# Mixture-of-experts slots behind cross-attention: two slots between stages, twelve row buffers, plans moved or split, and sends ahead of scatters on POOL

## The reference

```python
def _L0_xattn_ref(src, tgt, src_mask, tgt_mask, W_src, b_src, W_tgt, b_tgt, W_out, b_out):
    ...
    scores = jnp.einsum('bthd,bshd->bhts', q, k) / np.sqrt(HEAD_DIM)
    scores = jnp.where(src_mask[:, None, None, :] == 0, -jnp.inf, scores)
    attn = jax.nn.softmax(scores, axis=-1)
    tgt_update = jnp.einsum('bhts,bshd->bthd', attn, v).reshape(b, t, OUT_SIZE)
    cat_tgt = jnp.concatenate([tgt, tgt_update], axis=2)
    return jnp.einsum('btf,of->bto', cat_tgt, W_out) + b_out
def _L0_ffn_ref(x, router_w, w1, w2):
    ...
    probs = jax.nn.softmax(xf @ router_w.T, axis=-1)
    topv, topi = jax.lax.top_k(probs, 2)
    topv = topv / (topv.sum(axis=-1, keepdims=True) + 1e-09)
    cw = (jax.nn.one_hot(topi, e, dtype=xf.dtype) * topv[..., None]).sum(axis=1)
    h = jax.nn.gelu(jnp.einsum('td,edh->teh', xf, w1), approximate=False)
    y = jnp.einsum('teh,ehd->ted', h, w2)
    out = jnp.einsum('te,ted->td', cw, y)
...
x = x + jnp.tanh(g_xattn[0]) * _L0_xattn_ref(ctx_2048, _layernorm(x, axis=-1), mask_BxS2_fk1, ...)
x = x + jnp.tanh(g_ffn[0]) * _L0_ffn_ref(_layernorm(x, axis=-1), ...)
```

## Time and profile before

| | us |
|---|---|
| median of 3 executions | 447.37 (446.19 to 448.81) |
| the profiled execution, whole | 448.54 |
| its span, first to last instruction | 446.7 |
| PE busy | 369.7 (83%) |
| DVE busy | 227.2 (51%) |
| ACT busy | 183.3 (41%) |
| POOL busy | 268.4 (60%) |
| mean granted clock of PE | 0.938 |

### The profile page before, as it was taken

One profiled execution on the slowest core, in us unless ns is written; L12 is line 12 of the kernel. 1 busy time (PEld: TensorE's weight loads), 2 busy tenths in 40 slices (PEclk: granted clock), 3 DMA queues, 4 the chain that ended last, 5 costly groups with the idle time before them and its releaser, 6 DMA issues.

```text
span 446.7 us, 9992 instructions
## 1 busy us (share of the span) xinstructions
PE 369.7 (83%) x3067; PEld 304.4 (68%) x3067; DVE 227.2 (51%) x884; ACT 183.3 (41%) x428; POOL 268.4 (60%) x355
## 2 busy tenths in 40 slices
PE   0699999998999999999547878769766999999960
PEld 0566666676666667676336768769766999999960
DVE  1435345667778687777571534324225333365323
ACT  2164544554554555544323524423222444444420
POOL 2446354642787878868350785775855665677560
PEclk9899999998999999999855999989968999999995
DMA  7213330202122111760112121221212223743306
GB/s 212 64 38 116 117 112 26 71 25 61 32 71 63 44 47 44 194 133 25 51 54 54 56 61 55 72 61 52 75 51 81 66 69 105 238 116 111 82 13 212
DMA packets 44323, 36.04 MB, mean 81 GB/s; under 512 B 5426, under 2 KB 40151, under 8 KB 44272
## 3 DMA queue, kind: packets, MB, share of 16 engines
q1 hardware_dynamic: 35504, 24.83, 20.2%
q0 software_dynamic: 4544, 8.47, 5.7%
q10 hardware_dynamic: 4224, 2.10, 1.7%
HBM read 22.82 MB, written 13.47 MB: 81 GB/s over the span
## 4 chain that ended last, share of the span: by engine, by line
PE 67%; issue 14%; DVE 6%; POOL 4%; DMA 4%; SPq 1%; another core or an unknown queue 1%; ACT 1%; DVEq 0%; POOLq 0%
PE ps_ts L1245 17%; PE ps_proj L1256 8%; PE ps_o L1256 8%; PE ps_st L1085 5%; PE ps_st L1088 5%; PE ps_o L1176 3%; PE ps_proj L1132 3%; PE ps_proj L1136 2%; PE ps_ts L1102 2%; DVE x2n L998 2%; PE ps_tail L1163 2%; PE ps_ts L1106 2%; PE ps_tail L1154 2%; DMA maskn<-mask 2%; DVE tw L848 1%
## 5 line engine op out<-in xcount | busy, mean ns | idle before, releaser
L1245 PE MATMUL ps_ts<-xt,w1c 128*128 128x128 f32 x624 | 87.7, 286 | 10.4 <-issue 8.2
L1245 PEld LDWEIGHTS ps_ts<-xt,w1c 128*128 128x128 f32 x624 | 79.8, 200 | 12.1 <-issue 9.2
L598 POOL DMA_INDIRECT picked<-yo,xg x78 | 79.0, 1013 | 13.1 <-POOL pscratch L588 8.5
L710 ACT ACTIVATE probT<-ps_ts 128x512 f32<-128x512 f32 x78 | 46.5, 597 | 66.2 <-PE ps_ts L1245 43.4
L565 POOL DMA_INDIRECT rows<-xr,posi x64 | 63.3, 989 | 16.1 <-issue 15.8
L539 POOL TENSOR_TENSOR kblk<-kT,headcol 128x512 fp32r<-128x512 f32 x32 | 33.3, 1040 | 52.5 <-ACT kT L645 52.3
L588 POOL TENSOR_TENSOR pscratch<-minus_half 1x1 f32<-1x1 f32 x102 | 26.9, 264 | 54.1 <-DVE yo L1041 49.9
L946 DVE TENSOR_REDUCE rowmax<-ps_ts 128x8 fp32r<-128x1024 f32 x32 | 39.1, 1221 | 36.5 <-PE ps_ts L1106 36.5
L1088 PEld LDWEIGHTS ps_st<-negident,rowmax 128*128 128x128 f32 x256 | 30.9, 189 | 24.3 <-issue 24.3
L632 ACT ACTIVATE probT<-ps_st,pencol 128x1024 f32<-128x1024 f32 x32 | 35.6, 1113 | 27.7 <-PE ps_st L1088 27.0
L1256 PE MATMUL ps_o<-w2s,probT 128*128 x312 | 43.2, 283 | 4.3 <-issue 4.3
(11 more groups left out here) (141 smaller groups left out, 626.1 us busy)
## 6 DMA issues: line engine op xcount, KB each, us to landing
xg<-rows SPq DMA_DIRECT2D x78, 65.0 KB
ctxs<-ctxT SPq DMA_DIRECT2D x32, 128.0 KB, 2.1
xs<-x SPq DMA_DIRECT2D x8, 256.0 KB
w1s<-w SPq DMA_DIRECT2D x4, 512.0 KB, 3.6
w2s<-w SPq DMA_DIRECT2D x8, 256.0 KB
maskbc<-picked SPq DMA_DIRECT2D x4, 512.0 KB
out<-xs ACTq DMA_DIRECT2D x8, 256.0 KB
maskbc<-mask SPq DMA_DIRECT2D x6, 256.0 KB
```

The costliest lines, as they stand in the source:

```text
L598: nc.gpsimd.indirect_dma_start(out=picked, out_offset=bass.IndirectOffsetOnAxis(ap=xg[:, r, D + 1:D + 2].bitcast(I32), axis=0), in_=yo[:, ...
L710: nc.scalar.activation(hid[:, j % 2, :, :], heads(ps_score[j % 2][:, :]), ACT.Gelu).then_inc(f_gelu, 1)
L1245: last = nc.tensor.matmul(ps_score[j % 2][:, c * 128:(c + 1) * 128], w1c[:, j % 2, c * 128:(c + 1) * 128], xt[:, j % XRING, :], start=True ...
```

## The change

- `RING` goes from 8 to 12; the register batches stay at eight (`REGS`).
- `LAG_UP` goes from 1 to 2 and `LAG_DOWN` from 2 to 4. `w1c`, `ps_score` and `hid` have three buffers (`DEEP`); the third `ps_score` is a half of `ps_st`, the others of `hid` come from the second half of `probT`'s heads. `ps_y` and the banks of T stay at two. `each_slot` runs two slots more to drain.
- plan(0) stands at the end of DVE's step (9, 1), plan(1) is cut in four pieces that run before slots 33, 34, 35 and 36.
- SP's second pads are issued one by one, each behind a load of slots 39 to 46.
- In the mixed steps POOL runs the three slots' sends first and the step's own work, the scatters, second.

```diff
-RING = 8
+RING = 12
+REGS = 8
 XRING = 4
-LAG_UP = 1
-LAG_DOWN = 2
+LAG_UP = 2
+LAG_DOWN = 4
+DEEP = 3
...
+PLAN_AT = PER * (GROUP * (DRAINED - TAIL) - 1)
...
-def each_slot(step, slot):
+def each_slot(step, slot, slots_first=False):
...
-            step(g, k)
+            if not slots_first:
+                step(g, k)
             for j in range(j, j + PER):
                 slot(j)
             j += 1
+            if slots_first:
+                step(g, k)
...
-        w1c = sb("w1c", [128, 2, HID])
+        w1c = sb("w1c", [128, DEEP, HID])
...
-        hid = probT[:, :, 0:HCH, :]
+        hid = probT[:, :, :, :].rearrange("p r (a c) t -> p (r a) c t", c=HCH)
...
-        ps_score = [ps_ts[:, 0:512], ps_ts[:, 512:1024]]
+        ps_score = [ps_ts[:, 0:512], ps_ts[:, 512:1024], ps_st[:, 512:1024]]
...
-            pads(0)
+            sp.wait_ge(s_plan, PAD_ROWS)
+            for e in range(EXPERTS):
+                pad(0, e)
             scattered(0)
-            for j in range(SLOTS_A - RING):
+            for j in range(SLOTS_A - EXPERTS):
                 load(j)
-            pads(1)
-            for j in range(SLOTS_A - RING, SLOTS_A):
-                load(j)
+            sp.wait_ge(s_plan, PLAN + PAD_ROWS)
+            for e in range(EXPERTS):
+                load(SLOTS_A - EXPERTS + e)
+                pad(1, e)
             scattered(1)
...
             each_step(step)
-            each_slot(step, slot)
+            each_slot(step, slot, slots_first=True)
...
-                    wait(act, f_down, j - 1)
-                    nc.scalar.activation(hid[:, j % 2, :, :], heads(ps_score[j % 2][:, :]),
+                    wait(act, f_down, j - DEEP + 1)
+                    nc.scalar.activation(hid[:, j % DEEP, :, :], heads(ps_score[j % DEEP][:, :]),
                                          ACT.Gelu).then_inc(f_gelu, 1)
...
-                if (g, k) == (TAIL - 1, 1):
-                    plan(0)
-                    nc.vector.memset(before[:, :], 0.0).then_inc(s_reset, 1)
-                if (g, k) == (DRAINED - 1, 3):
-                    plan(1)
...
+                if (g, k) == (TAIL - 1, 1):
+                    counted, spread, passed, placed_slots = plan(0)
+                    counted()
+                    spread()
+                    passed()
+                    placed_slots()
+                    nc.vector.memset(before[:, :], 0.0).then_inc(s_reset, 1)
+                if (g, k) == (DRAINED - 1, 3):
+                    second_plan[:] = plan(1)
...
             def slot(n):
+                if 0 <= n - PLAN_AT < 4:
+                    second_plan[n - PLAN_AT]()
                 j = slot_of(n, 0)
...
-                    wait(dve, f_up, j - 1)
+                    wait(dve, f_up, j - DEEP + 1)
...
-                    wait(pe, f_gelu, j - 1)
+                    wait(pe, f_gelu, j - DEEP + 1)
```

More of the change, by code:

```diff
@@ L459, in _, with pad @@
                              padrow[:, :].unsqueeze(1).broadcast_to([128, SPARE, ROW])).then_inc(s_pads, 16)
[L461 to L466, removed]
+            def pad(part, e):
+                r = row_of(pad_row[0:1, part, e:e + 1], EXPERTS * REGION - 128)
+                sp.dma_start(rows[bass.ds(r, 128), :], padrow[:, :]).then_inc(s_pads, 16)
             def scattered(part):
@@ L901, in then @@
                     dve.wait_ge(s_plan, PLAN * part + at[0])
[L903 to L911, removed]
@@ L912, in plan @@
-                then(nc.vector.tensor_reduce(nslots[:, :], more[:, :, :], AX.X, ALU.add))
-                then(nc.vector.tensor_tensor(
-                    upto[:, :, :], below,
-                    nslots[:, :].unsqueeze(1).broadcast_to([128, EXPERTS, EXPERTS]), ALU.mult))
-                then(nc.vector.tensor_reduce(ends[:, :], upto[:, :, :], AX.X, ALU.add))
-                then(nc.vector.tensor_tensor(
-                    past[:, 0:count, :], iota[:, 0:count].unsqueeze(2).broadcast_to([128, count, EXPERTS]),
-                    ends[:, :].unsqueeze(1).broadcast_to([128, count, EXPERTS]), ALU.is_ge))
@@ L934, in plan, with counted @@
-                assert at[0] == PLAN
+                def counted():
+                    dve.wait_ge(s_total, part + 1)
+                    then(nc.vector.tensor_copy(total[:, :], total_at[:, 0:EXPERTS]))
+                    then(nc.vector.tensor_tensor(prow[:, :], total[:, :], regions[:, part, :], ALU.add))
+                    then(nc.vector.tensor_copy(pad_row[:, part, :], prow[:, :]))
+                    then(nc.vector.tensor_scalar(srow[:, 0:BATCH], iota[:, 0:BATCH], 128.0, None, ALU.mult))
@@ new lines, in spread @@
+                def spread():
+                    then(nc.vector.tensor_tensor(
+                        more[:, :, :], total[:, :].unsqueeze(2).broadcast_to([128, EXPERTS, BATCH]),
+                        srow[:, 0:BATCH].unsqueeze(1).broadcast_to([128, EXPERTS, BATCH]), ALU.is_gt))
+                    then(nc.vector.tensor_reduce(nslots[:, :], more[:, :, :], AX.X, ALU.add))
+                    then(nc.vector.tensor_tensor(
+                        upto[:, :, :], below,
+                        nslots[:, :].unsqueeze(1).broadcast_to([128, EXPERTS, EXPERTS]), ALU.mult))
+                    then(nc.vector.tensor_reduce(ends[:, :], upto[:, :, :], AX.X, ALU.add))
@@ new lines, in passed @@
+                def passed():
+                    then(nc.vector.tensor_tensor(
+                        past[:, 0:count, :], iota[:, 0:count].unsqueeze(2).broadcast_to([128, count, EXPERTS]),
+                        ends[:, :].unsqueeze(1).broadcast_to([128, count, EXPERTS]), ALU.is_ge))
+                    then(nc.vector.tensor_tensor(
+                        gone[:, 0:count, :], past[:, 0:count, :],
+                        nslots[:, :].unsqueeze(1).broadcast_to([128, count, EXPERTS]), ALU.mult))
+                    then(nc.vector.tensor_reduce(sexp[:, 0:count], past[:, 0:count, :], AX.X, ALU.add))
+                    then(nc.vector.tensor_reduce(sgone[:, 0:count], gone[:, 0:count, :], AX.X, ALU.add))
@@ new lines, in placed_slots @@
+                def placed_slots():
+                    then(nc.vector.tensor_tensor(srow[:, 0:count], iota[:, 0:count], sgone[:, 0:count], ALU.subtract))
+                    then(nc.vector.tensor_scalar(sgone[:, 0:count], srow[:, 0:count], 128.0, float(START_OF[part]),
+                                                 ALU.mult, ALU.add))
+                    then(nc.vector.scalar_tensor_tensor(slot_row[:, mine], sexp[:, 0:count], float(REGION),
+                                                        sgone[:, 0:count], ALU.mult, ALU.add))
+                    then(nc.vector.tensor_scalar(slot_exp[:, mine], sexp[:, 0:count], float(EXPERTS - 1), None,
+                                                 ALU.min))
+                    assert at[0] == PLAN
```

34 lines of the change are left out of this document (12 added, 22 removed).

## The result

Timed beside each other, the kernel before took 446.8 us (median; 445.1 to 448.8) and the changed kernel 431.7 (429.0 to 433.6): a ratio of 0.966, with a 95% interval of 0.958 to 0.973. The predicted time was 425.6 (414 to 440). The profiled execution of after has a span of 428.3 us for the 446.7 of before; the prediction's sum had 425.0.

The account below looks back on a forecast made before the run. PE was taken as the bound, with 37 us of the mixed stage in reach. 446.7 of span less 3.1, 6.2 and 12.4 gave 425.0, or 425.6 us against the median; range 414 to 440 for eight in ten.

Parts of the forecast that it names:

- plan(0), 3.1 us: Start of slots: plan(0) behind the step's other DVE work brings slot 0's transpose to 235.0, gaining 3.1 us (1.1 to 6.7).
- plan(1), 6.2 us: Plan(1) held DVE in one piece; four pieces between slots gain 6.2 us (3.8 to 6.3) of PE idle and slow clock.
- part 3: One more slot of lag between stages covers late releases and DVE's step work in the mixed stage: 12.4 us (5 to 22).
- late releases: Gelu and eviction waits on PE without a releaser in the trace: some 20 us, 10 to 13 recovered (4 to 20).
- register loads: Loads of the experts' registers on PE every eighth slot: 0.5 to 0.9 us each, four in the mixed stage, kept.
- rank and transposes: Rank matmuls and one set of transposes wait for DVE in the same step, about 2.4 us in sum, kept.
- Filling costs nothing: Deeper pipeline: PE issues the same groups, two ups and four downs now lying behind the mixed stage, at no cost.
- The ring, 0 us: Twelve row buffers take out unevenness between POOL and PE, even at slot 43; nothing charged beyond part 3.
- The end, 16 us: The last 16 us, gathers, additions and stores without PE work, stay as they are.
- What I said would show it: Signs: slot 0 at 235, mixed stage 88 us, clock 0.95, no PE idle over 1.5 us at slots 32 to 36.
- Releases from PE come only when POOL pauses: Slower rival: a ring of twelve takes POOL's pauses away, deciding from about 37 unbroken DMAs; 464 us, chance 0.06.
- POOL keeps most of it: Rival: POOL becomes the bound, sends perhaps held 0.4 us by weight copies; 427, or 436 with late releases; chance 0.14.

Follow-up runs that it names:

- no_sends: Changed kernel with POOL's sends of slots 0 to 31 left out, a 0.2 us carrier in their place: 410.7 us, 0.918 of before.
- old_lags: Changed kernel with LAG_UP, LAG_DOWN and DEEP put back to 1, 2 and 2, all else kept: 445.0 us beside 446.7, 0.995.
- ring8: Changed kernel with RING 8 again for 12, all else kept: 445.9 us, 0.999 of before.
- pool_busy: Changed kernel with each send of slots 0 to 31 replaced by 1.04 us of plain POOL work: 420.6 us, 0.938 of before.
- spaced_sends: Changed kernel with some 0.5 us of plain POOL work put behind each send of slots 0 to 31: 442.0 us, 0.986 of before.
- ring16_rank: Changed kernel with 16 buffers, POOL's step work first as before, rank matmuls behind two slots of the step: 406.7 us beside 430.0, 0.946.
- plan0_alone: Kernel before with only plan(0) moved behind the other DVE work of its step: 426.3 us beside 430.0, 0.990.

## Why the prediction was right, and where its steps were not

**plan(0), 3.1 us: right.** Slot 0 comes at 234.97 for 235.0, and alone, on a chip of the second kind, the move brings 2.8 to 5.9 us.

**plan(1), 6.2 us: the mis-sized term.** Undone, it costs 0 to 2 us (0.964 for 0.966, whose intervals are 3 and 7 us wide; 1.8 us by the last down groups). The two intervals together allow some 3 us at most, less than the lower bound of 3.8. The step that failed was to add it to part 3. The 3.85 us stall of the earlier trace rows was one of a pipeline with one slot of cover; with two, and with releases that are late at the same slots, most of the split's gain is, as I read it, part 3's already; plan(1)'s split without the lag was not run. My ends of 3.8 and 6.3 were both the price in the old pipeline.

**Part 3, 12.4 us: 17 to 19, with other contents.** The span's 18.4 are net of 2.6 and 0.8 that are lost (below); less plan(0)'s 3.1 and plan(1)'s 0 to 1.8 it leaves 16.9 to 18.7 for the lag and the ring. 4.0 of them are the register loads of the pure stage and 2 to 3.6 those of the mixed one, so 9 to 13 us are left for the late releases, what they entail and DVE's steps, about what I had forecast (10 to 13, and 1 to 2). That is a remainder and was not measured by itself. By the mechanism it was cover and nothing else: the late releases did not become fewer (30.1 us for 25.5), PE's idle time did. Of the 7.9 us for the rank most are late releases too, with 1.9 left of them in no_sends; I had kept 2.4 for rank and transposes in sum, though before's trace already had 3.45 and 0.88 for the rank and 0.63 for the transposes. What I had kept by mistake were the register loads: they no longer stop PE in the pure stage, 60.9 to 56.9 us for the last 30 slots, 4.0 us, and old_lags brings them back (60.8). I took the 0.5 to 0.9 us for a price that every pipeline pays. They are only the idle time in it: eight slots of before with a load among them take 15.9 to 16.5 us, where 15.2 is the full pace, so a load costs 1.0 us in the mean, and with two slots of lag that is gone.

**"Filling costs nothing": wrong by 2.6 us.** From slot 77's transpose to the last down group it takes 6.4 us and not 3.7. I had two more down groups "behind the mixed stage" and never put them in the sum, since the 88 us of the stage were already without them.

**The ring, 0 us: wrong as a price, harmless in the sum.** I asked whether POOL would hold a buffer too long, and found that it would not; I didn't ask how long a buffer is out once the lag is four slots. ring8 answers: with 8 the lag's whole gain is gone. POOL's order moved nothing, as costed.

**The end, 16 us: 16.6, 0.8 more than before.** The last three sends follow each other at 1.35 us, and the first row block of the last gather is waited for 7.69 us, 7.01 before.

**What I said would show it.** Slot 0 at 235: so. Mixed stage 88: 88.5. Mean clock 0.95: 0.90; besides the slow start the granted clock still falls to half at 255, 286 and 317, each time at or just behind a stop of PE. No idle over 1.5 us and no loss of clock at slots 32 to 36: the longest idle time in PE's timeline is 0.92, but slot 33's up group is torn into three and the slot takes 5.6 us for 1.9, and the fall of clock at 317 lies there. That is a late release and not plan(1). Gelus 5 us late: the longest waits are 4.0 us for a Gelu and 5.1 for an eviction, so only just not. PE waiting for row loads at slots 40 to 46: it doesn't. POOL over nine tenths occupied: behind its first send at 243.1 it waited 9.1 us for DVE in 80, so just under. The pure pace of 1.90 held, and the end took 16.6 us for 16.

**The rivals.** "Releases from PE come only when POOL pauses" was the slower one, with 0.06. On the chips of the prediction the runs bear its mechanism out: no_sends and pool_busy take most of it away, and in spaced_sends it is weak with the pauses and strong without. Its price was wrong: a row of 37 DMAs without a pause didn't come about (the longest has 8), as POOL still waited 7.3 us for evictions behind its first send. "POOL keeps most of it" had the copies of the weights hold each send for 0.4 us, after the section "SBUF: two separate sides" of the Trainium skill's "SBUF — State Buffer". The sends took 1031 ns in the mean in after's stage and 1022 where PE, DVE and POOL were densest (ring16_rank). Of ring16_rank's 78 sends 47 overlap a copy, and these take 1.03 us in the mean; a full lock at each would show, and beyond single sends of 1.2 to 1.3 us none does.

The forecast came out 6.1 us low, 3.3 of it in the profiled span: 4.4 to 6.2 for plan(1), 2.6 for the filling and 0.8 for the end, less 4.5 to 6.3 that part 3 brought above its 12.4. The rest is that the profiled execution of after was one of its quicker ones: the median stands 3.4 us over its span, where for before it stood 0.7 over. So the table of starts shows 18.4 us of gain where the medians have 15.1.

## What to carry over

A deeper pipeline is lag and buffers together: count how long a buffer is out (here some 17 us), divide by the pace, and that is the ring; with either alone next to nothing was won (0.995 and 0.999, against 0.966 with both). A stall that a deeper pipeline covers can't be counted a second time for the edit that removes it. A wait that has no releaser in the trace deserves its own experiment before it gets a price, and that experiment belongs on more than one chip. And the sum of such waits is not their price: it rose here while the time fell.

## What of the hardware was not expected

- On the chips where before takes 447 us ACT and DVE go on up to 7.3 us late behind PE, and up groups are torn into pieces, while POOL issues indirect DMAs 1.3 to 1.4 us apart without a pause. Plain POOL work of the same length does much less of it (2.9 us of such waits for 19.4), as do no sends at all (6.6), the same bytes sent by SP (6.8) and sends 2.1 us apart (5.5).
- On the two others the same unbroken rows do nothing, and before takes 430 us for 447. The late releases, which I had put at some 20 us, are the only difference that the traces show (slots 0 to 36 take 87.1 us in plan0_alone and 106.7 in before's trace); before itself has no trace from there.
- The traces differ in one more thing. The page's list of DMA issues gives the median time to landing of the row loads in all four traces of the second kind and in none of the ten of the first. These are no_sends, on a chip of the first kind, and ring16_rank:

```profile
xg<-rows SPq DMA_DIRECT2D x78, 65.0 KB
```
```profile
xg<-rows SPq DMA_DIRECT2D x78, 65.0 KB, 1.8
```

  On the first kind records of landings are missing from the trace. A link between lost records and engines held up is conceivable: the Trainium skill ("NOTIFIC — the notification-queue block", section "Overflow: three behaviours, one of which stalls the engine") states that, by its setting, a full queue of the recording block drops the new record, overwrites the oldest, or stalls the engine that makes them. No run here tested that. Every execution on record has a recorded span, so none tells whether the late releases are there when nothing is recorded. Whether the missing records and the late releases have one cause, and what distinguishes the chips, stays open; so does what the changed kernel gains on a chip of the second kind, where it wasn't run.
- In before, with one slot of lag, the register load of eight experts between slots lasts 1.93 to 2.34 us on PE, with idle time behind it; in after, with two, it lasts 0.59 to 0.72 us and PE doesn't stand.
